# First stage of a Mamba-and-FFN kernel: statistics ahead of splits, loads after the input, butterflies behind the groups

## The reference

```python
x = x + 0.5 * ffn(layernorm(x))
x = x + attn(layernorm(x))          # a Mamba-2 mixer: in-projection, convolution, chunked scan, gate, out-projection
x = x + 0.5 * ffn(layernorm(x))

def ffn(x):                          # HIDDEN 512, INTER 2048
    x = fwht(x * SU_ug) / 64         # Walsh-Hadamard transform over the 512 features
    up, gate = x @ W_up.T * (Wscale * 64), x @ W_gate.T * (Wscale * 64)
    x = fwht(silu(gate) * up * SU_dp) / 64   # over 2048
    return x @ W_down.T * (Wscale_dp * 64)
```

## Time and profile before

| | |
|---|---|
| median of 3 runs | 1694.22 us (1693.03 to 1702.69) |
| the profiled execution | 1699.64 us, of which the span is 1697.5 us |
| TensorE busy | 1633.7 us, 96% of the span |
| VectorE, ScalarE, GpSimd busy | 1032.5, 630.3 and 378.4 us |
| mean granted TensorE clock | 0.991 of full |

### The profile page before, as it was taken

How to read it: one execution, slowest core, us unless ns; L and a number is a source line. 1 busy time by engine, 2 the same in 40 slices (tenths; PEclk the granted TensorE clock), 3 DMA queues, 4 the chain that set the end, 5 groups by cost and what they waited for, 6 DMA issues and landing times.

```text
span 1697.5 us, 25014 instructions
## 1 busy us (share of the span) xinstructions
PE 1633.7 (96%) x9672; PEld 1317.8 (78%) x9672; DVE 1032.5 (61%) x2022; ACT 630.3 (37%) x936; POOL 378.4 (22%) x298
## 2 busy tenths in 40 slices
PE   6899999898999999999999999999999999999998
PEld 3677777676888877888877888877888887887886
DVE  6634444576667676677777777677677664443333
ACT  4333333345333355234355333345343332112111
POOL 3356662011212112122222131221222130000000
PEclk9999999999999999999999999999999999999999
DMA  8656654454445535545444445445444447566563
GB/s 254 235 187 235 227 200 180 184 175 144 155 151 165 162 113 169 170 143 174 152 144 153 147 163 162 163 139 186 142 163 158 157 127 221 164 191 191 179 206 112
DMA packets 253427, 290.46 MB, mean 171 GB/s; under 512 B 14464, under 2 KB 211200, under 8 KB 244096
## 3 DMA queue, kind: packets, MB, share of 16 engines
q1 hardware_dynamic: 253312, 288.88, 51.8%
HBM read 238.51 MB, written 50.33 MB: 170 GB/s over the span
## 4 chain that ended last, share of the span: by engine, by line
PE 62%; DVE 11%; ACT 3%; issue 2%; POOL 0%; DVEq 0%; ACTq 0%; POOLq 0%
PE bank L1113 25%; PE bank L1154 14%; PE bank L1076 10%; PE bank L1170 4%; PE bank L1239 2%; DVE m_cv L1696 2%; PE bank L1226 2%; PE bank L1188 1%; DVE m_sta L1740 1%; PE bank L1210 1%; DVE m_sta L1742 1%; DVE xn L1669 1%; PE bank L1198 1%; DVE m_mv L164 1%; ACT m_hb L1455 1%
## 5 line engine op out<-in xcount | busy, mean ns | idle before, releaser
L1113 PE MATMUL bank<-fxT,wj 128*128 128x512 f32 x1992 | 471.2, 390 | 2.3 <-DVE fxT L1662 1.5
L1113 PEld LDWEIGHTS bank<-fxT,wj 128*128 128x128 f32 x1992 | 373.8, 188 | 80.9 <-DVE res L1681 3.1
L1154 PE MATMUL bank<-m_wd,m_hb 128*128 128x512 f32 x1152 | 287.6, 395 | 6.6 <-DVE m_hb L1675 6.2
L1154 PEld LDWEIGHTS bank<-m_wd,m_hb 128*128 128x128 f32 x1152 | 214.2, 189 | 54.1 <-issue 11.7
L1076 PE MATMUL bank<-xT,wi 128*128 128x512 f32 x912 | 227.1, 397 | 3.2 <-DVE m_cv L1696 2.1
L1455 ACT CAST m_hb<-xn 128x512 fp32r<-128x512 f32 x96 | 59.5, 620 | 449.8 <-DVE xn L1669 449.8
L1076 PEld LDWEIGHTS bank<-xT,wi 128*128 128x128 f32 x912 | 169.0, 189 | 41.5 <-issue 5.8
L1681 DVE TENSOR_TENSOR res<-bank,res 128x512 f32<-128x512 f32 x192 | 132.5, 690 | 90.8 <-PE bank L1154 89.9
L1994 POOL TENSOR_TENSOR m_L<-m_L,m_GT 128x512 f32<-128x512 f32 x36 | 52.8, 1468 | 459.4 <-ACT m_L L1464 459.4
L1669 DVE SCALAR_TENSOR_TENSOR xn<-bank,sc,xn 128x512 f32<-128x512 f32 x96 | 71.7, 747 | 131.0 <-PE bank L1113 130.9
L1449 ACT ACTIVATE xn<-bank,sc 128x512 f32<-128x512 f32 x96 | 66.0, 688 | 141.0 <-PE bank L1113 137.5
(11 more groups left out here) (210 smaller groups left out, 2169.7 us busy)
## 6 DMA issues: line engine op xcount, KB each, us to landing
wj<-ug_split SPq DMA_DIRECT2D x167, 512.0 KB, 4.2
m_wd<-dn_split SPq DMA_DIRECT2D x48, 1024.0 KB, 4.9
wi<-in_split SPq DMA_DIRECT2D x76, 512.0 KB, 3.3
ug_split<-b_wu SPq DMA_DIRECT2D x8, 2048.0 KB, 14.2
m_wo<-out_split SPq DMA_DIRECT2D x32, 512.0 KB, 4.1
wi<-ug_split SPq DMA_DIRECT2D x25, 512.0 KB, 4.2
in_split<-b_msp SPq DMA_DIRECT2D x20, 512.0 KB, 3.7
raw<-in_wug SPq DMA_DIRECT2D x8, 1024.0 KB, 7.0
```

The costliest lines, as they stand in the source:

```text
L1113: ins = pe.matmul(to[:], w[:, a, k, :], fxT[:, b, k, :], start=(k == 0 and i == 0), stop=(k == KH - 1 and i == 2))
L1154: ins = pe.matmul(F[t % 2][:], hb[:, a, j, ck(t)], wd[:, b, j, :], start=(j == 0 and n == 0), stop=(j == 1 and n == 2))
```

## The change

It reorders instructions in `begin` and changes no arithmetic: the products, splits and transfers are the same in number and size.

1. **VectorE, statistics.** `bn_stats` of sequence 0 no longer waits for sequence 1's load; `roots` and `bias` come directly behind the statistics, ahead of the four low halves of ("ug", 0, k).
2. **SyncE, loads.** After the two input loads SyncE waits for the first to land, then issues groups 4 to 11, `fetch(1)`, groups 12 to 15.
3. **TensorE, ScalarE and VectorE, groups.** TensorE takes groups 8 and 9 behind the transposes of sequence 0 instead of ahead, 10 to 12 behind up(0, 0) and 13 to 15 behind up(0, 1); the other two engines follow.
4. **Units 0 and 1.** The six weight turns there are all in unit 1, in pairs behind up(1, 1), up(1, 2) and up(1, 3).
5. **GpSimd.** Chunk 1's butterflies wait for VectorE's last scaled group (`s_gw` at 8). In the loop the second half for chunk c + 2 runs one unit later, in the odd unit.
6. **The last weight blocks.** Blocks 26 and 27 are split by ScalarE behind the last two `rows`, `hidden_high` and two turns, and by VectorE between two turns and the adds of unit 15; before, both engines did them at the start of unit 15.

```diff
@@ turns and unit_turns
-                + [("ug", 1, 0), ("ug", 1, 1), ("ug", 1, 2), ("dn", 0, 0), ("dn", 0, 1), ("ug", 1, 3)]):
+                + [("ug", 1, 0), ("dn", 0, 0), ("ug", 1, 1), ("dn", 0, 1), ("ug", 1, 2), ("ug", 1, 3)]):
-                return (), (("x", 1, 0), ("x", 1, 1)), (("x", 1, 2), ("x", 1, 3)), (("ug", 1, 0), ("ug", 1, 1))
+                return (), (("x", 1, 0), ("x", 1, 1)), (("x", 1, 2), ("x", 1, 3)), ()
-                return (("ug", 1, 2),), (("dn", 0, 0),), (("dn", 0, 1),), (("ug", 1, 3),)
+                return (), (("ug", 1, 0), ("dn", 0, 0)), (("ug", 1, 1), ("dn", 0, 1)), (("ug", 1, 2), ("ug", 1, 3))
@@ sync
-            for i in range(4, FB):
+            sp.wait_ge(s_x0, 16)
+            for i in range(4, 12):
                 load_group(i)
             fetch(1)
+            for i in range(12, FB):
+                load_group(i)
@@ gpsimd
-            pool.wait_ge(s_b0, 4)
-            pool.wait_ge(s_mv, 1)
+            pool.wait_ge(s_gw, FB // 2)
             butterflies(1, False)
             butterflies(1, True)
             for c in range(NC):
                 if c + 2 < NC:
                     butterflies(c + 2, False)
-                    butterflies(c + 2, True)
                 for g in range(2):
+                    if g and c + 2 < NC:
+                        butterflies(c + 2, True)
@@ tensor
-            for i in range(4, 10):
+            for i in range(4, 8):
                 group(i)
             for t in range(TPG):
                 turn(("x", 0, t))
-            group(10)
-            group(11)
+            group(8)
+            group(9)
...
-                        group(12 + 2 * j)
-                        group(13 + 2 * j)
+                        for i in range(10 + 3 * j, 13 + 3 * j):
+                            group(i)
@@ scalar
-            for i in range(4, 8):
-                group(i)
+            group(4)
+            group(5)
             rows(0)
-            group(9)
             for t in range(TPG):
                 turn(("x", 0, t))
-            group(11)
+            group(6)
+            group(7)
+            group(9)
             rows(1)
...
-            high_blocks(UNITS - 1)
             silu(UNITS - 1, 0)
             silu(UNITS - 1, 1)
             rows(3, (0, 1))
             hidden_high(UNITS - 1, 0)
             rows(3, (2, 3))
             hidden_high(UNITS - 1, 1)
-            for t in range(TPG):
-                turn(("x", 3, t))
+            turn(("x", 3, 0))
+            turn(("x", 3, 1))
+            high_blocks(UNITS - 1)
+            turn(("x", 3, 2))
+            turn(("x", 3, 3))
@@ vector
-            both = stats(0, 2 * TPG, 0)
-            dve.wait_ge(s_x0, 16)
-            dve.wait_ge(s_x1, 16)
-            next(both)
+            for landed, c in ((s_x0, 0), (s_x1, 1)):
+                dve.wait_ge(landed, 16)
+                for t in range(TPG * c, TPG * c + TPG):
+                    own.done(dve.bn_stats(st[:, t, :], res[:, t, :]))
+            roots(dve, st, mv, own)
+            bias(0, 2 * TPG)
             for k in range(KH):
                 turn(("ug", 0, k))
-            next(both)
-            bias(0, 2 * TPG)
-            group(8)
             for t in range(TPG):
                 turn(("x", 0, t))
-            group(10)
-            for i in (4, 5, 6, 7, 9, 11):
+            for i in (8, 4, 5, 6, 7, 9):
                 group(i)
...
             n = UNITS - 1
-            low_blocks(n)
...
-            for t in range(0, TPG, 2):
-                turn(("x", 3, t))
-                turn(("x", 3, t + 1))
-                add(n, (t, t + 1))
+            turn(("x", 3, 0))
+            turn(("x", 3, 1))
+            low_blocks(n)
+            add(n, (0, 1))
+            turn(("x", 3, 2))
+            turn(("x", 3, 3))
+            add(n, (2, 3))
```

More of the change, by code:

```diff
@@ L640, in _ @@
                 if n == 0:
+                    group(11)
                     group(13)
@@ L778, in _ @@
                 if n == 0:
-                    group(12)
-                    group(13)
+                    for i in range(10, 14):
+                        group(i)
                 for key in keys[0]:
```

## The result

| | before | after |
|---|---|---|
| median of the comparison, us | 1694.62 (1693.03 to 1702.69, 4 runs) | 1681.32 (1676.78 to 1683.41, 4 runs) |
| profiled execution, us | 1699.64, span 1697.5 | 1676.78, span 1674.8 |
| clock of the profiled execution | 0.991 | 0.996 |

The changed kernel takes 0.9901 of the time before (95% interval 0.9877 to 0.9924): 13 us less. The forecast was 1672.5 us with a range up to 1681; the median is 8.8 us above the forecast and 0.3 us above the range. The two profiled executions differ by 22.9 us, close to the 21.9 of the sum, but that of after was the fastest of its runs, and that of before lies 5 us over its median. So the first question is why the traces agree with the sum and the medians don't.

What follows compares the result with a forecast made beforehand. TensorE, busy for 96% of the span, was taken as the bound, so only its holes cost time. From the median, 11.1 + 4.1 + 6.7 = 21.9 us off gave 1672.5 us, range 1668 to 1681.

Steps and rivals of the forecast that it cites:

- A: First stage: an earlier root and groups scaled without GpSimd beside them shrink TensorE's two holes; gain 11.1 us.
- B: Units 4 to 10: moving GpSimd's second butterfly half shrinks four holes ahead of `down`'s second half; gain 4.1 us.
- C: Unit 15: moving the last weight blocks out of VectorE's way removes the 5.40 us hole; mixer starts 6.7 us earlier.
- R1: Unit 1: down weights land late and TensorE's queued turn stops the units behind it; 2.3 us lost, 1675 us; 20%.
- R2: First stage: the chain to up(0, 2) ends 4 to 6 us later; gain 16 to 18, 1676 to 1679 us; 12%.
- R3: Units 4 to 10: moved half meets another two-input instruction, or DRAM wait sets unit 6; gain there 0 to 1, 1676; 5%.
- R4: Chunks 3 to 7: GpSimd's moved butterfly half becomes a new wait and makes the kernel slower; 3%.

Runs made afterwards that it cites:

- again: The changed kernel run once more without an edit, against the kernel before: 1681.31 us, ratio 0.9898.
- blocks_early: The changed kernel with the last weight blocks one place earlier on ScalarE and VectorE, between the halves of unit 15's silu and hidden: 1676.26 us, ratio 0.9871.
- down_first: The changed kernel with only the 1 MB store of down weights 7 moved ahead of the last two block stores: 1676.39 us, ratio 0.986.
- both_early: The changed kernel with the edits of blocks_early and down_first together: 1676.1 us, ratio 0.9868.
- fetch1_early: The kernel before with one DMA moved, `fetch(1)` issued ahead of groups 12 to 15: 1691.7 us, ratio 0.9956.
- c_only: The kernel before with only the last weight blocks moved (point 6): 1690.39 us, ratio 0.9968.
- b_only: The kernel before with only the second half of GpSimd's butterflies one unit later: 1696.69 us, ratio 0.9982.
- a_only: The kernel before with points 1 to 4 and chunk 1's butterflies behind the groups; second butterfly halves and last blocks left in place: 1687.36 us, ratio 0.994.
- root_behind: The changed kernel with VectorE's low halves of up weights 0 ahead of the statistics' root again: 1684.77 us, ratio 0.9903.
- no_sp_wait: The changed kernel without SyncE's wait for the first rows of x ahead of groups 4 to 11: 1680.66 us, ratio 0.9884.
- pool_early: The changed kernel with GpSimd's old gate, chunk 1's butterflies not waiting for VectorE's groups: 1687.0 us, ratio 0.9931.
- gate_only: The kernel before with only GpSimd's first butterflies made to wait for VectorE's last scaled group: 1696.65 us, ratio 0.9992.

## Why the prediction was right, and where it was off

**The sum.** Against the profiled execution it gave 1677.7 us; the profiled execution of after took 1676.8. Per term: A 12.9 for 11.1, B 4.2 for 4.1, C 5.5 for 6.7. The mechanisms are the ones forecast, but so close a match is part luck: A's excess hides C's shortfall, and the traced execution of after was the fastest of eight, with no slow products at the switch. The stated median, 1672.5, was 8.8 us too low.

**A** held step by step: ScalarE's rows at 24.5 (25.0 forecast), up(0, 2) at 42.9 (44.2), `down(0)` at 65.2 (67.1). Two small things made it better: both loads landed 0.7 to 0.8 us earlier than in before, and TensorE, without the long hole, did the transposes in 1.09 us instead of 1.97. In the five traces with all of points 1 to 5 in full (after, again, blocks_early, down_first, both_early) `down(0)` lies between 65.2 and 67.7 us; half of that spread is the first landing, 9.1 to 10.5 us. What the forecast did not see: A's gain depends on the execution of before it is held against, 12.9 us against the bad outcome of its first stage, some 4 against the good one (69.1 in fetch1_early, 69.7 in c_only). That the traced execution of before had the usual outcome was not known. Within A the gate, the early `fetch(1)` and the root have runs of their own; the order of the groups and turns (points 3 and 4) has none.

**B** is confirmed by b_only, where the loop gains 4.1 us, and by the eight other traces with the moved half: from the first `down` to unit 14's they take 249.3 to 250.3 us.

**C is the term that was mis-sized.** The forecast gave the two stores "some 3.7 us and up to 1 us more: zero to 0.5 us" at the end. It overlooked that `keep_down(7)` stands between them on the queue: the mixer started 1.9 us behind the last addition in after, where before has 0.33 us and the forecast allowed at most 0.5 more. I had moved the block stores to the end of the program without walking SyncE's list past them. In three of six traces that have this order the mixer starts 1.5 us later than in down_first, in the other three 3.4; in five of the six the mixer itself is longer than down_first's, by 2.3 to 3.2 us. The forecast had called a mixer changed by more than 2 us the sign that it is wrong at its root. The root was not wrong, as the mixer does the same work, but the premise that it "only starts sooner" was: those five are the ones whose granted clock fell at the switch. The median pays 4.9 us (1681.3 against 1676.4). Without it the term was better than forecast: 25.0 us from unit 14's `down` to the mixer, 7.1 gained.

**The base.** 1672.5 came from the median of three runs, 1694.22. I noted that the profiled execution stood 5.4 us above it and took the median all the same. Over 62 more runs the median is 1699.2: the profiled one was the typical one. 1699.2 less the sum is 1677.3; with the 4.9 us of the switch 1682.2, and measured is 1681.3. Both errors, 5.0 and 4.9 us, had the same sign.

**Rivals.** R1, the late down weights, appeared with the new order in two traces, at 0.78 us in again and 0.16 us in a_only, and not in after. R2 and R3 did not happen, nor R4.

## What to carry to other kernels

Where an edit pushes a transfer towards a point at which all engines wait, write down everything that stands in front of it on the issuing engine, with bytes; a store that was hidden becomes the last thing on the path. Before taking off a sum from a median of three, take more runs and see how they lie: here a race between one landing and another engine's order gave first stages 8.5 us apart, b_only's runs form two groups and before's spread over 15.5 us, and removing the race (one `fetch` four places earlier) was worth 7.5 us with nothing else changed. And a gate that keeps two engines apart pays only together with an order that no longer asks early for what the gated engine makes.

## What the runs showed of the hardware

A 0.5 MB store that landed in 2.6 to 2.7 us with little in flight took 5.6 to 7.5 us behind 1 MB issued 0.5 us earlier on the same engine (after, again, c_only, root_behind, no_sp_wait); the megabyte itself landed in 4.8 us in after and 5.5 in again.

VectorE's 128x512 multiply with both inputs in SBUF took 0.68 to 0.69 us alone in after and 1.5 to 2.9 us beside GpSimd's butterflies in pool_early, two kernels that differ only in the gate.

The granted clock falls at some holes. Over 341 to 352 us its mean was 0.84 in again, where the hole of 4.52 us ends inside the stretch, and 1.00 in down_first; the columns are the stretch, its length, TensorE's busy time, its clock, the DMA share and GB/s:

```profile
341.00:352.00 11.00, 6.48 (x24) 0.84 0.25 85
```

```profile
341.00:352.00 11.00, 10.15 (x45) 1.00 0.45 139
```

Over the first 8 us of the mixer the mean is 0.82 in again: 2.9 us of them at the lower level, 1.2 GHz, and the rest at 2.4, if only these two occur (an estimate from the mean). That would cost 1.4 us, which is what its first 24 products took longer.

The length of the hole alone does not decide it: after, c_only and pool_early all had 2.6 us, and over the first 8 us of the mixer 1.00, 0.82 and 0.79. It does sort the mixers. The nine with 1.00 there (before, after, a_only, b_only, fetch1_early, gate_only, blocks_early, down_first, both_early) take 1333.7 to 1335.1 us, the five with 0.79 to 0.82 take 1336.7 to 1337.6. So after has the shortest of the six because its clock held. What decides that is open. The first 24 products account for 1.4 to 1.6 us of the difference; where the rest arises was not looked into.
